# Attention stage of a two-branch layer: memory read on row tiles, paired A/B products, and a new order of the queues

## The reference

```
xn = layernorm(x)                      # [8192, 512]
Q, K, V = xn @ Wq.T, xn @ Wk.T, xn @ Wv.T      # 16 heads of 32, segments of 64 tokens
M = 0 (32x32 per head); z = 0
for each of the 128 segments:          # sq = elu(q)+1, sk = elu(k)+1
    A_mem = (sq @ M) / (sq . z + 1e-6)
    A_dot = softmax(causal(q @ k.T / sqrt(32))) @ v
    out   = sigmoid(beta) * A_mem + (1 - sigmoid(beta)) * A_dot
    V_prev = (sk @ M) / (sk . z + 1e-6)
    M = M + sk.T @ (v - V_prev);  z = z + sum(sk)
result = x + concat(out) @ Wo.T + selected_tokens_block(xn)
```

## Time and profile before

| | us |
|---|---|
| median of 3 runs | 2214.99 |
| the profiled execution | 2217.72 |
| its span, first to last instruction | 2216.0 |
| PE busy | 2032.5 (92%) |
| DVE busy | 1441.5 (65%) |
| ACT busy | 902.9 (41%) |
| POOL busy | 396.0 (18%) |
| mean granted clock of PE | 0.969 of full |

### The profile page before, as it was taken

One profiled execution on the slowest core, in us unless ns is written; L12 is line 12 of the kernel. 1 busy time (PEld: TensorE's weight loads), 2 busy tenths in 40 slices (PEclk: granted clock), 3 DMA queues, 4 the chain that ended last, 5 costly groups with the idle time before them and its releaser, 6 DMA issues. The chain is left out here.

```text
span 2216.0 us, 67517 instructions
## 1 busy us (share of the span) xinstructions
PE 2032.5 (92%) x29628; PEld 1696.0 (77%) x29628; DVE 1441.5 (65%) x3475; ACT 902.9 (41%) x1568; POOL 396.0 (18%) x700
## 2 busy tenths in 40 slices
PE   4999999999999999999999998349899999987998
PEld 4888888888888888888888887237677777766897
DVE  5666666676667667666666665577577777785322
ACT  3344334333334343333433433214476666654110
POOL 1222222222222222222222222141100000000100
PEclk9999999999999999999999999569899999998999
DMA  3111111111111111111111110215400000004100
GB/s 120 31 31 50 36 36 36 50 36 31 55 36 31 50 41 31 50 40 32 49 37 36 35 42 26 77 57 176 147 11 11 11 11 11 11 1 152 48 10 20
DMA packets 61043, 100.02 MB, mean 45 GB/s; under 512 B 4608, under 2 KB 25104, under 8 KB 60752
## 3 DMA queue, kind: packets, MB, share of 16 engines
q1 hardware_dynamic: 54976, 76.56, 11.4%
q0 software_dynamic: 5776, 19.15, 2.8%
HBM read 51.13 MB, written 27.26 MB: 35 GB/s over the span
## 5 line engine op out<-in xcount | busy, mean ns | idle before, releaser
L335 POOL TENSOR_TENSOR Mbd<-M,headmask 128x128 f32<-128x128 f32 x512 | 231.7, 483 | 639.8 <-DVE M L600 637.1
L343 POOL TENSOR_TENSOR As<-T 128x512 f32<-128x512 f32 x64 | 93.8, 1465 | 419.1 <-DVE T L616 419.1
L1900 DVE CUSTOM_DVE_ANT_0 Sm<-Sp,mc 128x1023 f32<-128x1023 f32 x128 | 155.7, 1217 | 15.0 <-PE Sp L1942 7.6
L1804 ACT ACTIVATE Sm<-Sm,mxs 128x1023 f32<-128x1023 f32 x128 | 147.0, 1149 | 36.6 <-DVE mxs L1902 36.4
L1970 PE MATMUL Op<-PTs,V 128*32 128x128 f32 (+1 forms) x2048 | 125.6, 276 | 0.9 <-DVE PTs L1851 0.9
L1942 PE MATMUL Sp<-KS,QS 128*128 128x512 f32 x256 | 95.1, 454 | 31.2 <-DVE mxs L1902 31.2
L590 DVE TENSOR_REDUCE mx<-S 128x16 f32<-128x1024 f32 x64 | 78.1, 1220 | 61.9 <-PE S L823 61.8
L1970 PEld LDWEIGHTS Op<-PTs,V 128*32 128x32 f32 (+1 forms) x2048 | 108.1, 111 | 12.1 <-issue 10.4
L1851 DVE COPY PTs<-Tp 128x512 f32<-128x512 f32 x128 | 88.6, 692 | 42.9 <-PE Tp L1954 42.8
L399 ACT ACTIVATE Pq<-Pq 128x1024 f32<-128x1024 f32 x64 | 68.6, 1072 | 107.3 <-DVE Pq L593 107.3
L363 ACT ACTIVATE PT<-S 128x1024 f32<-128x1024 f32 x64 | 65.7, 1026 | 113.2 <-PE S L873 113.2
(11 more groups left out here) (316 smaller groups left out, 5092.4 us busy)
## 6 DMA issues: line engine op xcount, KB each, us to landing
VS<-DV SPq DMA_DIRECT2D x64, 264.0 KB, 3.7
xin<-in_x SPq DMA_DIRECT2D x32, 512.0 KB, 4.7
out_rows<-outt SPq DMA_DIRECT2D x64, 256.0 KB, 2.0
mask_columns<-x1T SPq DMA_DIRECT2D x16, 512.0 KB
xs<-in_w SPq DMA_DIRECT2D x16, 512.0 KB, 4.7
QT<-in_wqT SPq DMA_DIRECT2D x1, 1024.0 KB, 10.9
KT<-in_wkT SPq DMA_DIRECT2D x1, 1024.0 KB, 13.1
SQT<-in_wvT SPq DMA_DIRECT2D x1, 1024.0 KB, 15.3
```

Of the source, the lines that this page charges most:

```text
L335: ins = pool.tensor_tensor(Mbd[:, 1 - b, g, :].rearrange("p (j d) -> p j d", j=J), bm(M[:, 1 - b, g, :], J), bc(headmask[:, :], DK), ALU.mult)
L343: pool.tensor_tensor(As[:, :], T1[:, :], T2[:, :], ALU.add).then_inc(s_as, 1)
L1804: act.activation(Sm[:, h % 4, 0:KC], Sm[:, h % 4, 0:KC], ACT.Exp, bias=mxs[:, h % 4, 1:2], accum_out=rsum[:, b, h:h + 1]).then_inc(s_e, 1)
L1900: link(dve.tensor_tensor_reduce(Sm[:, h % 4, 0:KC], Sp[h % 2][:, 0:KC], mc[:, b, 0:KC], 1.0, -3.0e38, ALU.add, ALU.max, mxs[:, h % 4, 0:1]))
```

## The change

- `memory` no longer needs the block diagonal: it multiplies head by head with M itself, 32 matmuls on tiles of 32 rows and 64 columns, and writes into the half of `S` that the other row tile uses. M gets four slots, one per segment. `Mbd`, `AM`, `diagonal` and their semaphore go; POOL is left with `rows`.
- `a_and_b` works both segments of a row tile in one call. The two segments lie on different row halves of the array and alternate there; each has a bank of its own. `neg_a` copies both at once.
- In PE's queue, `pv`, `scores` and the projections `feature` and `values` are no longer cut into pieces. `p_transposes` stands right behind `a_and_b`, ahead of the output product and of `values`. `memory` waits for `softmax_part` of its row tile (s_t1), the mask for `memory_part` (s_t2).
- In DVE's queue, `softmax_part` of row tile 0 stands behind the first M update, `row_max` and `less_max` of row tile 1 follow each other, `low_a` comes behind them, and `deviation` behind the first sigma of K. In ACT's queue, `prob` of row tile 1 stands ahead of the second K projection's part.

```diff
-        M = sb("M", [P, 2, G, DK])
-        Mbd = sb("Mbd", [P, 2, G, P])
+        M = sb("M", [P, SEGS, G, DK])
...
-        AB = ctx.enter_context(nc.psum_tensor("AB", [P, 2, G, 2, DK], F32))
-        AM = ctx.enter_context(nc.psum_tensor("AM", [P, 512], F32))
+        AB = ctx.enter_context(nc.psum_tensor("AB", [P, 2, 2, G, 2, DK], F32))
...
                 for a in range(TILES):
-                    diagonal(m * SEGS + 2 * a, 0)
                     rows(m * 2 + a, m, a)
-                    diagonal(m * SEGS + 2 * a + 1, 1)
...
-            def neg_a(m, sg):
-                act.wait_ge(s_ab, m * SEGS + (sg + 1))
-                copy(NA[:, sg % 2, :, :], AB[:, sg % 2, :, 0, :]).then_inc(s_na, 1)
+            def neg_a(m, a):
+                act.wait_ge(s_ab, m * 2 + (a + 1))
+                copy(NA[:, :, :, :], AB[:, :, 0, :, 0, :]).then_inc(s_na, 1)
...
                 dve.wait_ge(s_am, m * 2 + (a + 1))
-                dve.tensor_tensor(T2[:, :].rearrange("p (h d) -> p h d", h=H),
-                                  AM[:, :].rearrange("p (h d) -> p h d", h=H),
...
+                R = S[:, :, (1 - a) * 256:(1 - a) * 256 + G * DK].rearrange("p j (g d) -> p j g d", g=G)
...
-            def a_and_b(m, p, sg):
-                a, b = sg // 2, sg % 2
-                if sg == 0:
+            def a_and_b(m, p, a):
+                if a == 0:
                     pe.wait_ge(s_dsk, m * 2 + 2)
-                pe.wait_ge(s_m, m * SEGS + sg + 1)
+                pe.wait_ge(s_m, m * SEGS + 2 * a + 1)
...
                 for g in range(G):
                     for j in range(J):
                         h = g * J + j
-                        ins = pe.matmul(AB[DK * j:DK * j + DK, b, g, :, :], SK[t, p, a, h * DK:h * DK + DK],
-                                        DV[t, p, a, :, h, 0:DK], start=g == 0, stop=g == G - 1,
-                                        skip_group_check=True)
+                        for b in range(2):
+                            t = slice(b * SEG, b * SEG + SEG)
+                            ins = pe.matmul(AB[DK * j:DK * j + DK, b, 0, g, :, :], SK[t, p, a, h * DK:h * DK + DK],
+                                            DV[t, p, a, :, h, 0:DK], start=g == 0, stop=g == G - 1,
+                                            skip_group_check=True)
...
             def memory(m, p, a):
-                t = a * P
-                pe.wait_ge(s_mbd, m * SEGS + 2 * a + 2)
-                pe.wait_ge(s_t2, m * 2 + a + 1)
+                pe.wait_ge(s_m, m * SEGS + 2 * a + 2)
+                pe.wait_ge(s_t1, m * 2 + a + 2)
                 for g in range(G):
+                    o = (1 - a) * 256 + g * DK
                     for b in range(2):
-                        ins = pe.matmul(AM[b * SEG:b * SEG + SEG, g * P:g * P + P],
-                                        SQT[:, p, g, t + b * SEG:t + b * SEG + SEG],
-                                        Mbd[:, b, g, :], start=True, stop=True)
+                        t = a * P + b * SEG
+                        for j in range(J):
+                            q = slice(DK * j, DK * j + DK)
+                            ins = pe.matmul(S[b * SEG:b * SEG + SEG, j, o:o + DK], SQT[q, p, g, t:t + SEG],
+                                            M[q, 2 * a + b, g, :], start=True, stop=True)
```

More of the change, by code:

```diff
@@ L329, in _ @@
             pool.wait_ge(s_const, 1)
-            def diagonal(s_no, b):
-                pool.wait_ge(s_m, s_no + 2)
-                for g in range(G):
-                    ins = pool.tensor_tensor(Mbd[:, 1 - b, g, :].rearrange("p (j d) -> p j d", j=J),
-                                             bm(M[:, 1 - b, g, :], J), bc(headmask[:, :], DK), ALU.mult)
-                ins.then_inc(s_mbd, 1)
             def rows(n2, m, a):
@@ L599, in m_next @@
                 dve.wait_ge(s_tm, m * SEGS + (sg + 1))
-                dve.tensor_tensor(M[:, 1 - b, :, :], AB[:, b, :, 1, :], M[:, b, :, :], ALU.add).then_inc(s_m, 1)
+                dve.tensor_tensor(M[:, (sg + 1) % SEGS, :, :], AB[:, b, 0, :, 1, :], M[:, sg, :, :],
+                                  ALU.add).then_inc(s_m, 1)
             def softmax_part(m, a):
@@ L651, in half @@
                     residual(pn)
+                memory_part(m, p, 0)
+                m_next(m, 1)
                 if ln:
@@ L655, in half @@
                     sigma(m, "QT", 1, SQT[:, pn, 2:4, :], s_sq)
+                row_max(m, 1)
+                less_max(m, 1)
+                low_a(m, m * 2, 0)
+                if stage1:
+                    sigma(m, "KT", 0, SKT[:, 0:2, :], s_sk)
                 if ln:
                     deviation()
-                softmax_part(m, 0)
-                memory_part(m, p, 0)
-                if stage1:
-                    sigma(m, "KT", 0, SKT[:, 0:2, :], s_sk)
-                m_next(m, 1)
-                row_max(m, 1)
-                low_a(m, m * 2, 0)
-                less_max(m, 1)
                 if stage1:
                     sigma(m, "KT", 1, SKT[:, 2:4, :], s_sk)
-                if stage1:
                     z_chain(m + 1, n2, pn)
@@ L851, in t_times_m @@
                         q = slice(DK * j, DK * j + DK)
-                        ins = pe.matmul(AB[q, b, g, 1, :], NA[q, b, g, :], M[q, b, g, :], start=False,
+                        ins = pe.matmul(AB[q, b, 0, g, 1, :], NA[q, b, g, :], M[q, sg, g, :], start=False,
                                         stop=g == G - 1, skip_group_check=True)
@@ L875, in p_transposes, with pv @@
                 ins.then_inc(s_ptp, 1)
-            def pv(m, mh, p, a, gs):
-                if gs[0] == 0:
-                    pe.wait_ge(s_pt, m * 2 + (a + 1))
-                    if a == 0:
-                        pe.wait_ge(s_vs[p], (mh + 1) * 32)
-                    alone(pe, s_alone_pe)
-                for g in gs:
+            def pv(m, mh, p, a):
+                pe.wait_ge(s_pt, m * 2 + (a + 1))
+                if a == 0:
+                    pe.wait_ge(s_vs[p], (mh + 1) * 32)
+                alone(pe, s_alone_pe)
+                for g in range(G):
                     for j in range(J):
@@ L918, in half @@
                 if stage1:
-                    feature(m, "QT", wq, 0, ("XT", None if m == 0 else m - 1), half=0)
+                    feature(m, "QT", wq, 0, ("XT", None if m == 0 else m - 1))
                 if not first:
                     as_transposes(m, m * 2 - 1, 1)
-                if stage1:
-                    feature(m, "QT", wq, 0, half=1)
                 a_and_b(m, p, 0)
+                p_transposes(m, 0)
                 if not first:
@@ L927, in half @@
                 t_times_m(m, 0)
[L928 removed]
+                pv(m, mh, p, 0)
                 if stage1:
                     feature(m, "QT", wq, 1)
[L931 to L937 removed]
                 memory(m, p, 0)
                 t_times_m(m, 1)
+                if stage1:
+                    feature(m, "KT", wk, 0)
                 mask(m, 1)
                 scores(p, 1, 0)
[L942 to L943 removed]
                 scores(p, 1, 1)
@@ L946, in half @@
                 if stage1:
-                    feature(m, "KT", wk, 1, half=1)
-                a_and_b(m, p, 2)
+                    feature(m, "KT", wk, 1)
+                a_and_b(m, p, 1)
+                p_transposes(m, 1)
                 if stage1:
                     values(m, 0)
-                p_transposes(m, 1)
                 t_times_m(m, 2)
+                pv(m, mh, p, 1)
                 if stage1:
-                    values(m, 1, (0, 1))
-                pv(m, mh, p, 1, (0, 1))
-                if stage1:
-                    values(m, 1, (2,))
-                pv(m, mh, p, 1, (2, 3))
-                a_and_b(m, p, 3)
+                    values(m, 1)
                 if stage1:
@@ L972, in half @@
                     scores(pn, 0, 0)
+                    scores(pn, 0, 1)
                 if ln:
                     x_transposes(m, m + 2, p, "XT", 1)
-                if stage1:
-                    scores(pn, 0, 1)
                 out_proj(m, 0)
```

38 lines of the change are left out of this document (11 added, 27 removed).

## The result

The changed kernel takes 2154.47 us against 2216.07 for the kernel before on the same chip: a ratio of 0.9718, 95% interval 0.9693 to 0.9743. It is 62 us faster. The median is over four runs, of which one was slow (2267.94 us at a granted clock of 0.832) and three lie between 2149.26 and 2154.76. Forecast were 2129, with 2113 to 2184 as the range. The profiled execution took 2154.18, its span is 2152.2, 63.8 less than before.

What follows compares the result with a forecast made beforehand. The tensor engine's own queue was taken to bound the attention stage; 3.30 us saved less 0.54 of waits gives 2.76 per pass, x 31 = 86 us, so 2129 us. Own range 2115 to 2145, wide range 2113 to 2184.

Steps and rivals of the forecast that it cites:

- The bound: Attention stage: the tensor engine's own queue sets the end; the feed-forward part behind it stays at 820 us.
- Steps 1 and 2: Attention pass: fewer small-tile entries save 0.45 us, fewer returns 0.55; PV and scores in fewer blocks save 0.26 each.
- Steps 3 and 4: A/B product and memory read on eight tiles, 0.65 us per block: 1.02 and 0.76 us saved per pass.
- My high end of 0.76: A/B block of 64 instructions: upper estimate, no fixed part and 12 ns for each instruction.
- Step 5: POOL's block diagonals removed, scalar's NA copies joined, Newton chain moved behind the second tile's maximum: 0 us by itself.
- Step 6: New waits of the tensor engine, its queue being shorter between producer and consumer: 0.54 us per pass.
- SK: Second four SK transposes, which need V's bank, wait for the scalar engine's copy of V: 0.49 us.
- The output product's 0.05: Output product of the row tile before waits 0.05 us for the low half: 2.17 us against 2.12 of queue.
- The chain of the second tile: Scores to row transposes: no wait, slack 0.07 us; as rival, vector engine 1.0 us later, 2160 us, 12%.
- Four tiles at a time: Rival, A/B and memory read: eight tiles worked like four, blocks 1.03 and 1.13 us, total 2181 us, 19%.
- Two at a time: Rival, eight-tile blocks: 32 ns per instruction, 8.2 us where now 4.4, total 2302 us, 5%; decided above 21 ns.

Runs made afterwards that it cites:

- the cut block: Changed kernel with each 64-instruction A/B block cut into two of 32, the eight row transposes between them: 2160.21 us, ratio 0.9752.
- the experiments that force it: Changed kernel with the two segments one after the other instead of alternating, in the A/B product (2164.19 us) or in the memory read (2159.71 us).
- the three edits to it: Changed kernel with low half of A between maximum and subtraction (2162.11 us), Newton chain ahead of the maximum (2171.00), or scores cut in two (2219.17).
- the cut of the scores: Changed kernel with row tile 1's scores cut in two again, half of the second K projection between them: 2219.17 us, ratio 1.0025.
- the repeat: The changed kernel itself, unedited, measured once more beside the others: 2149.95 us, ratio 0.9699 to the kernel before.

## Why the forecast was right, and where its terms were off

The direction, the mechanism (a shorter queue of the tensor engine) and the range of 2113 to 2184 were right. The gain was forecast at 86 us and came to 62, and 2154 lies outside my own range of 2115 to 2145; it is inside the wide one because that took in two of the rivals, neither of which came true. By the steps of the prediction, each per pass:

- The bound. Right: the tensor engine's queue sets the pass; the second branch stayed at 818 us.
- Steps 1 and 2, fewer entries and returns, PV and scores whole. PV gained the 0.26. The scores gained 0.51 where 0.26 was worked out, since 64 instructions in one piece take 1.00 where two pieces of 32 take 0.63 each; that the second column half starts while the first still works is likely, not shown. Entries and returns were not measured one by one. Their prices hold in the kernel after (the product behind the memory read, 633.00 to 633.57, takes 0.57 where the next takes 0.47), and by difference they gave 0.90 of the forecast 1.00.
- Steps 3 and 4, the eight-tile blocks. This is the mis-sized term: 0.79 rather than 0.65 in each of four. A/B saved 4 x 0.58 - 2 x 0.79 = 0.74 (1.02 forecast), the read 2 x 1.03 - 2 x 0.79 = 0.48 (0.76). Together 0.56 a pass short, 17 us. I had taken a rate from 32 instructions and carried it on to 64; the first 32 do start 8 ns apart, and the cut block shows that the second 32 are slow only in a row with the first. My high end of 0.76, L852's 12 ns for all 64, was the better reading, and still 0.03 low.
- Step 5. POOL's work went from 396 to 152 us and gave nothing by itself, as forecast. The Newton chain costs nothing where it stands; where it stood ahead of the maximum it costs 20 to 24 us.
- Step 6, waits. SK 0.42 (0.49 forecast), on the engine and the copy that were named. The output product's 0.05 isn't there. The chain of the second tile has 0.37 of slack where 0.07 was worked out; the A/B block in front, 0.14 longer than thought, gives part of it.
- Sum: 0.74 + 0.48 + 0.26 + 0.51 + 0.90 - 0.42 = 2.47, forecast 2.76. The 0.90 is what was left to reach 2.47, so the sum doesn't test itself. The difference is 9 us over 31 passes, and that it isn't the 17 of the mis-sized term is luck: the scores gave 0.25 a pass more than reckoned and the waits took 0.12 less.
- The term that was missing: 12 us, most of it from gaps in which PE waits for its own instructions (1.6 of it is the slow clock behind the longest gap, see the last section). The prediction had nothing for it. Nothing in the trace of before shows such a gap; the margin was there to be read (291 instructions where 449 are the end), and so was a burst of transfers beside a stretch that the change was to fill with more instructions. The 9 and the 12 us, with 0.5 at the ends, make the 22 us between the gain forecast (86) and the gain of the span (64).

The rivals. Four tiles at a time fell: the experiments that force it give 0.92 and 0.94 where the changed kernel has 0.79. The Trainium skill, "TensorE: Matmul & The Clock Gate", section Part 3, by which tiles beyond four still add, holds here in its direction (eight tiles are faster than four), but the gain is 0.13 us of 0.92 and 0.16 of 0.94. The chain of the second tile didn't bind, but the three edits to it show how near it is: 0.6 us more work on it costs 0.2 a pass, the Newton chain 0.88, the cut of the scores, with its other costs, 2.28. Two at a time fell outright: 0.79 / 64 is 12.3 ns an instruction, against 32 and a limit of 21. By "TensorEngine Tiling (Array Packing)", section Instruction Overhead, of the Trainium skill, the 32-column read would have gained nothing from its short rows. Here the trace looks like the rule, since this block and the A/B block with 64 moving columns both take 0.79. But the cut block puts that down to what comes behind the first 32 instructions, and in the earlier trace rows 32 instructions on four tiles cost 0.38 with 32 columns and 0.58 with 64.

## What to carry to other kernels

A rate per instruction read from a block of 32 small matmuls doesn't hold for 64 in a row; price the longer block by its slowest plausible rate. Putting something slow in its middle sped up its second half here and cost more than it gave. When a queue gets denser, look where its instruction fetches land and keep bursts of transfers away from there: moving copies and a load by some 9 to 12 us brought the last output product 7 to 9 us forward here. After such a change the slack of the chains behind it is small: each of the three edits to the second tile's chain cost the pass 0.2 to 2.3 us.

## What the runs showed of the hardware that was not expected

- Small matmuls on eight tiles start 8 ns apart on average for the first 32, and 12 ns apart for the next 31, at full granted clock (622.77 to 623.42).
- PE's program comes in pieces of 16 KB through a queue of its own, 259 of them, one per 127 matmuls with their loads. Between two of them 9.3 us passed (602.56 to 611.90), the last 4.2 of these with 551 data packets, and PE stood still for 2.48 us. All eight gaps opened at the same count of instructions (449 or 450, as above), and PE resumed 2.4 to 2.7 us after the fetch had begun.
- Such a gap can cost more than its length. In the first profile of the changed kernel the blocks right behind it ran slower (the fourth and fifth row of the gap's timeline above: 1.68 and 1.91 for four instructions, 1.18 in the repeat). The stretch behind the gap:

```profile
614.60:619.40 4.80, 4.80 (x20) 3.87 (x17) 3.05 (x3) 0.87 (x2) 0.00 (x0) 0.64 0.01 3
```

The granted clock is 0.64 of full there, that is, part of the stretch at 1.2 GHz and part at 2.4, after 2.48 us in which PE did nothing. In the repeat the same gap was followed by a full clock (1.00 from 614.90 to 619.40), so it doesn't always come.
